# Read-out factors of the state stage as constant products, tanh gates, a second transpose bank at the attention's layer ends, and new turn tables, in an eight-stage graph network

## What is computed

```python
# G0, three times
r = sigmoid(i_r + h_r); z = sigmoid(i_z + h_z); n = tanh(i_n + r * h_n)
h = (1.0 - z) * n + z * h
# F2, chunks of 128 nodes, four heads of 64
A_cum = cumsum(dA)
Y_diag = einsum('bcln,bcsn,bhcls,bcshp->bclhp', Cc, Bc, exp(segsum(dA)), xdt)
states = einsum('bcln,bhcl,bclhp->bchpn', Bc, exp(A_cum[..., -1:] - A_cum), xdt)
# prevs: the states before each chunk, by a scan over the chunks with factor exp(A_cum[..., -1])
Y_off = einsum('bcln,bchpn,bhcl->bclhp', Cc, prevs, exp(A_cum))
# G3, in each of two layers
attn = softmax(where(adj > 0, q @ k.T * scale, -1e9)); out = attn @ v
```

## Time and profile before

| | |
|---|---|
| three runs | 3577.15, 3580.18, 3581.81 us, median 3580.18 |
| profiled execution | 3579.64 us, its span 3577.6 us |
| busy in the span | PE 3110.6 us (87%), DVE 2287.5 (64%), ACT 1894.6 (53%), POOL 775.0 (22%) |
| mean granted clock of TensorE | 0.969 |

### The profile page before, as it was taken

How to read it: one execution, slowest core, us unless ns; L and a number is a source line. 1 busy time by engine, 2 the same in 40 slices (tenths; PEclk the granted TensorE clock), 3 DMA queues, 4 the chain that set the end, 5 groups by cost and what they waited for, 6 DMA issues and landing times.

```text
span 3577.6 us, 54364 instructions
## 1 busy us (share of the span) xinstructions
PE 3110.6 (87%) x20506; PEld 2085.0 (58%) x20506; DVE 2287.5 (64%) x7012; ACT 1894.6 (53%) x3318; POOL 775.0 (22%) x836
## 2 busy tenths in 40 slices
PE   8988988888888888988888888888988888888889
PEld 5755555555555555555555555555555565555577
DVE  3575756767566675756767566675666757566653
ACT  2246454654746546454664646546555664646534
POOL 0022112221222222112221222212122221222212
PEclk9999999999999999999999999999999999999999
DMA  3000000000000000000000000000000000000000
GB/s 126 1 18 1 7 15 4 18 1 21 1 7 16 1 21 1 7 15 4 18 1 20 2 4 18 1 21 1 7 16 4 18 1 7 1 4 3 1 7 5
DMA packets 28741, 40.15 MB, mean 11 GB/s; under 512 B 1344, under 2 KB 17728, under 8 KB 28224
## 3 DMA queue, kind: packets, MB, share of 16 engines
q1 hardware_dynamic: 28480, 36.67, 3.1%
HBM read 28.28 MB, written 4.19 MB: 9 GB/s over the span
## 4 chain that ended last, share of the span: by engine, by line
PE 63%; DVE 19%; ACT 11%; issue 5%; POOL 2%; DVEq 0%; ACTq 0%; POOLq 0%
PE ps L433 48%; PE ps L880 6%; ACT scratch L1044 6%; DVE scratch L1334 6%; PE ps L442 3%; DVE scratch L1340 3%; PE ps L1036 2%; ACT L1044 2%; DVE scratch L1820 2%; ACT adjf L1044 2%; POOL rstd L2023 2%; DVE stats L1355 1%; DVE scratch L1337 1%; DVE x L1340 1%; PE ps L612 1%
## 5 line engine op out<-in xcount | busy, mean ns | idle before, releaser
L433 PE MATMUL ps<-scratch 128*128 128x128 f32 (+6 forms) x4608 | 553.7, 386 | 114.3 <-DVE scratch L1334 45.6
L1044 ACT ACTIVATE scratch<-scratch 128x512 f32<-128x512 f32 (+4 forms) x768 | 527.9, 690 | 213.8 <-DVE scratch L1334 90.1
L433 PE MATMUL ps<-xT,weights_sb 128*128 128x512 f32 x1152 | 566.1, 603 | 32.6 <-ACT xT L1044 20.6
L2060 POOL TENSOR_SCALAR scratch<-scratch 128x512 f32<-128x512 f32 x512 | 360.9, 720 | 929.3 <-DVE scratch L1827 928.7
L433 PEld LDWEIGHTS ps<-scratch 128*128 128x128 f32 (+5 forms) x4608 | 347.0, 161 | 241.0 <-issue 88.3
L433 PE MATMUL ps<-weights_sb,scratch 128*128 128x128 f32 (+2 forms) x3456 | 480.9, 280 | 1.9 <-DVE scratch L1478 1.9
L433 PEld LDWEIGHTS ps<-weights_sb,scratch 128*128 128x128 f32 (+2 forms) x3456 | 430.9, 190 | 79.6 <-issue 47.0
L1044 ACT ACTIVATE scratch<-ps 128x512 f32<-128x512 f32 (+2 forms) x512 | 286.4, 568 | 287.3 <-PE ps L433 154.2
L880 PE MATMUL ps<-weights_sb,scratch 128*128 128x128 f32 x2048 | 323.3, 281 | 90.8 <-ACT adjf L1044 53.3
L2023 POOL TENSOR_TENSOR rstd<-ve,minus_half 128x4 f32<-128x4 f32 x126 | 142.2, 1128 | 1191.7 <-DVE ve L1337 1191.7
L1044 ACT ACT_TABLE_LOAD x293 | 375.9, 1283 | 20.3 <-PEq L250 15.3
(11 more groups left out here) (164 smaller groups left out, 4482.0 us busy)
## 6 DMA issues: line engine op xcount, KB each, us to landing
adj<-adj SPq DMA_DIRECT2D x16, 1024.0 KB, 5.6
weights_sb<-weights SPq DMA_DIRECT2D x1, 4605.0 KB, 19.6
x_in<-x SPq DMA_DIRECT2D x16, 256.0 KB, 2.8
scratch<-scratch SPq DMA_DIRECT2D x32, 128.0 KB, 2.3
out<-x SPq DMA_DIRECT2D x16, 256.0 KB, 2.3
scratch<-raw SPq DMA_DIRECT2D x1, 1645.0 KB, 22.9
weights_sb<-weights SPq DMA_DIRECT2D x1, 499.0 KB, 7.0
scratch<-raw SPq DMA_DIRECT2D x1, 384.0 KB, 5.3
```

The costliest lines, as they stand in the source:

```text
L433: return pe.matmul(o, lhsT, rhs, start=start, stop=stop, **k)
L1044: return act.activation(o, a, func, **k)
L2060: pool.tensor_scalar(p, p, cut(g, G3_RI + n, 1), 1.0, ALU.mult, ALU.mult).then_inc(s["att_p"], 1)
```

## The change

What it does, part by part. The factors exp(A_cum) of chunks 1 to 3 are no longer taken from the 16 transposed rows: 12 more matmuls (a column of sums, broadcast over 64 columns, times the identity, two heads in the two halves of the array) put them into bank `lp(4)` in the layout in which C is needed, ACT takes two exponentials (128x512 and 128x256), and one DVE product 128x768 makes the read-out factors for all partitions; GpSimd's two products are gone. DVE's differences no longer wait for ACT. The sigmoids of G0 are written with tanh, and the factors of one half go into biases, scales and DVE's three-operand instruction (same number and size of instructions). At the layer ends of G3 the odd turns 11, 13 and 15 use bank `lp(0)`. All turn tables are new.

```diff
-    "leeeeellllelllllleeeeeellllllllelleleeeeelelelleellllleeeeeeeeeellllllllelllleeeeellllelllleleeeelelee"
+    "eeleeeeellllelllllleeeelllllllleelleeeeeeleellllllllleleeeeeellleeelllllelllleeeeeeeeellelllellleele"
...
+                    yield from f2_reading(g, 1, 3)
+                def f2_reading(g, a, b):
+                    if a > 1:
+                        pe.wait_ge(*done("re_ready", g))
+                    for c in range(a, b):
+                        for k in range(2):
+                            for half in range(2):
+                                at = F2_S + 9 * 16 + c * MH + 2 * k + half
+                                to = (c - a) * MI + k * P
+                                last = mm(LP[4][half * MS:(half + 1) * MS, to:to + P], SC[g][:, at:at + 1].to_broadcast([P, MS]), ident,
+                                          tile_position=(0, half * MS))
+                    last.then_inc(s["gt_re_psum"], 1)
...
+                        if c == 3:
+                            yield from f2_reading(g, 3, T)
...
+            return 0 if n > 2 * AH + 2 and n % 2 else 4
...
+                    elif n == 2 * AH + 3:
+                        pe.wait_ge(*done("att_max", g, layer * T * AH + 3 * AH))
                     elif n >= 1:
-                        pe.wait_ge(*turned(layer, n - 1, g))
+                        pe.wait_ge(*turned(layer, n - 2 if n > 2 * AH + 2 else n - 1, g))
                     for j in range(T):
-                        last = pe.transpose(lp(4, P, P, j * P), probabilities(g, layer, n)[:, tile(j)], ident)
+                        last = pe.transpose(lp(turn_bank(n), P, P, j * P), probabilities(g, layer, n)[:, tile(j)], ident)
...
-                    f(cut(g, G0_R, N), ep(2), ACT.Sigmoid, bias=M("g0_brz")[:, 0:1]).then_inc(s["r_ready"], 1)
+                    f(cut(g, G0_R, N), ep(2), ACT.Tanh, scale=0.5, bias=M("g0_brz")[:, 0:1]).then_inc(s["r_ready"], 1)
...
-                    for n, c in enumerate((1, 2, 3, 0)):
-                        yield
-                        act.wait_ge(*done("row_psum", g, n))
-                        f(AF[g][:, c, :], lp(c), ACT.Exp).then_inc(s["re_ready"], 1)
+                    for n, width in enumerate((2 * MI, MI)):
+                        yield
+                        act.wait_ge(*done("gt_re_psum", g, 1 + n))
+                        f(AF[g][:, n, 0:width], lp(4, width), ACT.Exp).then_inc(s["re_ready"], 1)
...
-                    own(tt(u, u, r, ALU.mult))
+                    own(stt(u, r, 1.0, u, ALU.add, ALU.mult))
...
-                        v.wait_ge(*done("re_ready", g, n))
+                        v.wait_ge(*done("row_psum", g, n))
...
+                def f2_reading(g):
+                    v.wait_ge(*landed("cc_ready", g))
+                    v.wait_ge(*done("re_ready", g, 1))
+                    tt(ce, re, spread(cc, 2, [P, T - 1, 2, P]), ALU.mult).then_inc(s["ce_ready"], 1)
...
-                        pool.tensor_tensor(ce, re[rows, 1:T, half::2, :], spread(cc, 2, [MS, T - 1, 2, P]), ALU.mult).then_inc(s["ce_ready"], 1)
```

More of the change, by code:

```diff
@@ L804, in f2_across @@
                     yield
-                    pe.wait_ge(*done("ce_ready", g, 1))
+                    pe.wait_ge(*done("ce_ready", g))
                     for c in range(1, T):
@@ L1063, in g0_messages @@
                     act.wait_ge(*done("gate_psum", g, 4 * k + 0))
-                    f(cut(g, G0_U, N), ep(0), ACT.Identity, bias=W("g0_bhh")[:, 2:3]).then_inc(s["hn_ready"], 1)
+                    f(cut(g, G0_U, N), ep(0), ACT.Identity, scale=0.5, bias=M("g0_bhn")).then_inc(s["hn_ready"], 1)
                 def g0_gates(g, k):
@@ L1404, in g0_gates @@
                     own.wait()
-                    own(tt(r, r, z, ALU.mult))
+                    own(stt(r, z, 1.0, r, ALU.add, ALU.mult))
                     yield
                     own.wait()
-                    tt(h, u, r, ALU.add).then_inc(s["h_ready"], 1)
+                    stt(h, r, 0.5, u, ALU.mult, ALU.add).then_inc(s["h_ready"], 1)
                 def g0_end(g):
@@ L1763, in f2_state @@
                     v.wait_ge(*done("pv_zero", g))
+                    v.wait_ge(*done("re_ready", g))
                     for c in range(T - 1):
@@ L1779, in f2_state @@
                                 else:
-                                    h = 2 * k + half
-                                    last = stt(st, SC[g][rows, at - MI:at - MI + MD], AF[g][rows, c, h * P + P - 1:h * P + P], more, ALU.mult, ALU.add)
+                                    end = (c - 1) * MI + k * P + P - 1
+                                    last = stt(st, SC[g][rows, at - MI:at - MI + MD], AF[g][rows, 0, end:end + 1], more, ALU.mult, ALU.add)
                         last.then_inc(s["pv_ready"], 1)
@@ L1943, in f2 @@
                     yield from f2_rows(g)
+                    yield from f2_reading(g)
                     yield from f2_weigh(g)
@@ L2039, in g2_adjacency @@
                     pool.tensor_copy(AF[g][:, :, :], ADJ[g][:, :, :]).then_inc(s["adjf_ready"], 1)
-                def f2_reading(g):
-                    yield
-                    pool.wait_ge(*done("re_ready", g, T - 1))
-                    pool.wait_ge(*landed("cc_ready", g))
-                    pool.wait_ge(*done("pv_zero", g))
-                    re = AF[g][:, :, :].rearrange("p c (h n) -> p c h n", h=MH)
-                    for half in range(2):
-                        rows = slice(half * MS, (half + 1) * MS)
-                        cc = SC[g][rows, F2_CC + P:F2_CC + T * P].rearrange("p (c n) -> p c n", c=T - 1)
-                        ce = SC[g][rows, F2_CE:F2_CE + (T - 1) * MI].rearrange("p (c k n) -> p c k n", c=T - 1, k=2)
-                        pool.tensor_tensor(ce, re[rows, 1:T, half::2, :], spread(cc, 2, [MS, T - 1, 2, P]), ALU.mult).then_inc(s["ce_ready"], 1)
-                        pool.wait_ge(*done("ce_ready", g, half))
                 def g3_normalise(g, layer, n):
@@ L2090, in f2 @@
                     pool.memset(cut(g, F2_PV, (T - 1) * MI), 0.0).then_inc(s["pv_zero"], 1)
-                    yield from f2_reading(g)
                     yield
```

56 lines of the change are left out of this document (32 added, 24 removed).

## The result

The changed kernel takes 3495.57 us (median of 4 runs, 3494.78 to 3496.95), the kernel before beside it 3578.66 us; the ratio is 0.9767, with a 95% interval of 0.975 to 0.9784. That is 83 us less. The time is in the main case's own range of 3495 to 3530 us, but at its very edge.

A forecast was written before the change was run, and what follows sets the result against it. PE bounds most stretches examined in a middle half, DVE the one from 1090 to 1104.5. Gains 36 + 28.5 + 6.6 = 71 us off 3579.64 give 3508.5, as a median 3509 us; range 3465 to 3570.

The forecast's parts named there:

- main case: Terms 36 + 28.5 + 6.6 hold within their bounds: 3509 us, own range 3495 to 3530, chance 0.47.
- The DVE chain: Middle halves, XDD to r product: shorter and earlier without POOL's products beside it, about 2.4 us a half, 36 us.
- Read-out on PE and DVE: Twelve more matmuls a graph and DVE's 128x768 product are covered by waits: 0; uncovered 12 and 14 us.
- ACT's loads: 232 table loads for 293, saved mostly where PE is the bound: 0; at most 23 us gain or 19 loss.
- Layer ends of the middle halves: G3's turns with alternate banks no longer wait for the preceding copy: 1.9 of 2.2 us a half, 28.5 us.
- Layer ends of the last half: Two banks allow two turns per step: 3.3 us a layer, two layers, 6.6 us, bounds 0 and 7.1.
- The new tables: G3 starts about one expert later, three more hidden tiles ahead; moved work on nearly full PE costs nothing: 0.
- Rival 1: After `h_ready` in middle halves the clock stays up with shorter waits: 33 us more, 3476 us, chance 0.22.
- Rivals 2 and 3: 2: layer ends give nothing, experts pay, 3537 to 3556, 0.17; 3: POOL's products not slowing DVE, about 3580, 0.06.
- rival 4: G3's later start delays the late lane's end in each middle half: 91 us lost, 3600 us, chance 0.08.
- would show it: Expected profile signs, among them `h_ready` wait of 2.95 us down by 1 to 2.4, period some 210.5 us, 232 loads.

The follow-up runs named there:

- the last one: Changed kernel with both the CAST behind G1's layer norm and 36 small matmuls on PE ahead of the wait for `h_ready`: 3492.94 us, ratio 0.9751.
- the fillers: Changed kernel plus 36 small matmuls without result on PE ahead of its wait for `h_ready` in each middle half: 3471.01 us, ratio 0.9697.

## Why the prediction was right

*The DVE chain* (36 us, 2.4 a half): the mechanism was right. With the read-out part alone the stretch is shorter by 2.4 us, in the changed kernel by 3.0. Its price was a little high: at equal low time a half gains 1.9 us, and of the 40 us that this part gave some 12 go with the clock, which the term did not hold. Inside the term two errors cancel. I kept XDD at 2.13 us and gave the weighted halves 1.22 each; it is 0.96 and 3.44 together. XDD now starts just ahead of the CAST, and the CAST waits for it (2.54 for 1.89 us), then the first weighted half waits for the CAST. Which of the two waits depends on who starts first, and the sum did not ask that.

The Trainium skill, "SBUF — State Buffer", section "SBUF: two separate sides", says that whichever of the two engines starts first holds the shared ports for its whole instruction and the other waits. By that rule the CAST would end at 1068.34 + 1.89 = 1070.2 and the two weighted halves, which take 2.35 us together where no CAST is beside them, at 1072.6; the trace is near it (1070.09 and 1072.30). The rule was right about the mechanism, and my application of it to XDD was not, as XDD came first.

*Read-out on PE and DVE, at 0*: nearly. With the read-out part alone the last difference comes 46.13 us after the store, before 46.14; in the changed kernel 46.44, 0.3 us more. What the part costs behind `h_ready` is the 0.5 us above; PE is busy for 185.6 us in that half for 183.9.

*ACT's loads, at 0*: right, in the old order (+2 us, within the measurement) and in the new one (-1 us). 78 us of ACT's time were worth nothing.

*Layer ends of the middle halves* (28.5 us): the mechanism was right, the size depends on what else is there. Alone the second bank gives 13.6 us, 1.1 in the last half and the rest in the others, under 1 us a half for 1.9; behind the read-out part it gives 1.6 us a half, 24 us in 15. With the new tables it cannot be priced as a part at all: without it they lose 182 us.

*Layer ends of the last half* (6.6 us): 2 x 3.1 = 6.2 us, but only with the new table, which puts fewer fillers between the turns; the bank alone gives 1.1.

*The new tables, at 0*: wrong by 17 us, of which 7.9 lie in the last half (174.9 to 167.0 us) and are counted in the term before. In the 14 periods the tables gain 12 us, and 5.7 are lost before the first store. The 12 are the difference of two larger amounts. A half of the old order with 10.2 us low, to be compared with 1018.87:1226.91 above (10.3 us low):

```profile
1647.40:1858.40 211.00, 186.50 (x1184) 123.12 (x1186) 139.75 (x437) 112.90 (x202) 43.53 (x51) 0.98 0.03 10
```

At equal low time the new order is 3.0 us a half shorter, but the mean low time rises from 8.8 to 14.9 us and takes most of it back. PE's idle time is 24.5 us in both halves (29.6 in the kernel before, so that fall belongs to the parts and not to the order); the 3.0 us are busy time of PE, 183.6 for 186.5 us with the same matmuls. I had counted a move of work on a full PE as free. Why the same work takes less busy time in the new order was not traced.

*Rival 1, the clock*: it moved the wrong way in the changed kernel, where the low time a period rose from 12.2 to 14.9 us. With the read-out part alone, and with all parts in the old order, it fell to 8.8 us, as this rival has it; with the bank alone it did not (13.4). So it is the new tables that raised it. What it costs is seen where the same instructions run with different clocks: 208.0 us with 10.3 us low, 211.8 with 20.5, 215.0 with 27.3, about 0.4 us for each us low. (In other kernels the same comparison gives 0.3 to 0.5: 213.5 us with 6.8 and 216.8 with 17.1 in the kernel before, 205.8 with 6.8 and 214.0 with 23.9 in the last one.) So by that estimate the clock took some 1.1 us a half, 16 us, from the change. The main case gave the clock nothing; the fillers bring 25 us, where this rival had 33. Rivals 2 and 3 did not come, as the bank and the read-out each gave their gain, nor did rival 4.

So the sum came within 13 us with the right mechanisms for its terms, and in part by luck: the chain and the bank were priced too high, and the tables and the clock, which it left out, are larger than the 13 us and of opposite signs. Of what "would show it", the wait of 2.95 us fell to 2.90 only: PE reaches it earlier too, so its length says nothing of the gain; the place of `h_ready` in the half does. Two signs failed: XDD did not stay near 2.1 us, and the 128x1024 products did not come to 1230 ns but to 1.7 us each.

## What to carry to other kernels

Before a GpSimd instruction is put "where that engine is free", look at what DVE does at that moment: of two instructions that meet in SBUF one waits for the other, and here that wait fell on the engine that matters. Moving the CAST into DVE's idle time gave 15 us; moving it beside other DVE work lost 19. A part and the order that was made for it are to be tried together and apart: neither the bank (14 us) nor the tables (17 us behind all parts) show what the tables without the bank cost (182 us). With a TensorE that waits often, compare periods with their low-clock time beside them, or a gain of 1 us a half drowns in halves that differ by 8 us with the same instructions.

## What the runs showed of the hardware

DVE instructions with a single tensor operand that read and write SBUF (the layer norm's, L1363, with scalars from SBUF) are held up by GpSimd's CAST as well as those with two: four take 2.68 us for 1.12. A copy that reads PSUM is not (0.68 us beside the CAST). Where in a half the clock falls is not fixed by the half's instructions: the changed kernel's periods alternate between 208.0 and 211.8 us through the whole run, another execution of it starts with three of 215.0, and two changes that each gain 15 and 25 us can cost each other's gain. What makes it settle in one pattern or another was not found.
